# Third pair's weight sums, late x blocks and the typed stretch's x sums at other steps

## The reference, cut to what matters

```
x = x + L0(x)   # three shared relu MLPs 256->1024->256 on all tokens, two experts per batch chosen by its type,
                # a gate from the batch's first token mixes expert, s0, s1, s2
x = x + L1(x)   # eight weighted experts and one shared: (silu(x Wg) * (x Wu)) Wd, 256->1024->256
x = x + L2(x)   # adapter by language, 256->64->256, then layernorm
x = x + L3(x)   # matrix by subject, 256->256
```

## Time and profile before

| | |
|---|---|
| median of 3 runs | 1608.95 us (1607.98 to 1612.6) |
| the profiled execution's own time | 1607.21 us |
| its span | 1605.4 us, mean granted clock 0.997 |
| PE busy | 1583.1 us (99%), 7944 matmuls |
| PEld / DVE / ACT / POOL busy | 84% / 71% / 58% / 41% |

### The profile page before, as it was taken

One profiled execution on the slowest core, in us unless ns is written; L12 is line 12 of the kernel. 1 busy time (PEld: TensorE's weight loads), 2 busy tenths in 40 slices (PEclk: granted clock), 3 DMA queues, 4 the chain that ended last, 5 costly groups with the idle time before them and its releaser, 6 DMA issues.

```text
span 1605.4 us, 22399 instructions
## 1 busy us (share of the span) xinstructions
PE 1583.1 (99%) x7944; PEld 1346.5 (84%) x7944; DVE 1132.4 (71%) x1676; ACT 930.0 (58%) x1680; POOL 658.2 (41%) x576
## 2 busy tenths in 40 slices
PE   8999999999999999999999999999999999999999
PEld 6788888999897888888888888888888888888888
DVE  5665556788888776776776776776776777656556
ACT  4555554665666666666656656666666566554343
POOL 7665553745755441341341341341441431146110
PEclk9999999999999999999999999999999999999999
DMA  4111104555431010010010010010010010022000
GB/s 158 53 53 53 53 27 158 171 171 168 153 114 40 14 40 27 13 41 27 14 40 27 14 40 27 14 40 27 13 40 27 14 40 27 27 55 54 13 14 27
DMA packets 30500, 85.46 MB, mean 53 GB/s; under 512 B 5030, under 2 KB 10022, under 8 KB 30262
## 3 DMA queue, kind: packets, MB, share of 16 engines
q1 hardware_dynamic: 29798, 82.68, 15.7%
q0 software_dynamic: 304, 1.10, 0.2%
q10 hardware_dynamic: 288, 0.26, 0.1%
HBM read 81.93 MB, written 2.10 MB: 52 GB/s over the span
## 4 chain that ended last, share of the span: by engine, by line
PE 94%; DVE 3%; POOL 1%; issue 1%; ACT 1%; DMA 0%; SPq 0%; ACTq 0%; DVEq 0%; POOLq 0%
PE up L668 13%; PE up L669 13%; PE up L670 13%; PE sum L435 12%; PE sum L437 12%; PE sum L436 12%; PE up L435 4%; PE up L437 3%; PE up L436 3%; PE up L445 2%; PE up L443 2%; PE up L444 2%; DVE expert_out L2006 1%; DVE x L1988 0%; DVE hidden L2020 0%
## 5 line engine op out<-in xcount | busy, mean ns | idle before, releaser
L1267 ACT ACTIVATE hidden_hi<-up_tile 128x512 fp32r<-128x512 f32 x256 | 161.2, 630 | 187.3 <-DVE up_tile L2064 163.3
L2059 DVE TENSOR_TENSOR gate_tile<-up,gate_tile 128x512 f32<-128x512 f32 x192 | 130.0, 687 | 141.8 <-PE up L670 141.7
L2069 DVE TENSOR_TENSOR hidden_lo<-up_tile,hidden_hi 128x512 fp32r<-128x512 f32 x256 | 196.6, 787 | 44.7 <-ACT hidden_hi L1267 44.7
L668 PE MATMUL up<-x_sums,gate_up 128*128 128x512 f32 x512 | 199.3, 389 | 0.0
L437 PE MATMUL sum<-hidden_hi,down 128*128 128x512 f32 x512 | 199.2, 389 | 0.0
L435 PE MATMUL sum<-hidden_hi,down 128*128 128x512 f32 x512 | 199.2, 389 | 0.0
L436 PE MATMUL sum<-hidden_lo,down 128*128 128x512 f32 x512 | 199.2, 389 | 0.0
L670 PE MATMUL up<-x_sums,gate_up 128*128 128x512 f32 x512 | 199.2, 389 | 0.0
L669 PE MATMUL up<-x_sums,gate_up 128*128 128x512 f32 x512 | 199.2, 389 | 0.0
L2064 DVE TENSOR_TENSOR up_tile<-up_tile,gate_tile 128x512 f32<-128x512 f32 x192 | 183.5, 982 | 2.3
L1260 ACT ACTIVATE gate_tile<-gate_tile 128x512 f32<-128x512 f32 x192 | 119.8, 633 | 90.3 <-DVE gate_tile L2059 88.2
(11 more groups left out here) (323 smaller groups left out, 3956.9 us busy)
## 6 DMA issues: line engine op xcount, KB each, us to landing
raw<-in_experts SPq DMA_DIRECT2D x64, 512.0 KB, 3.3
raw<-in_l SPq DMA_DIRECT2D x51, 512.0 KB, 3.3
raw<-in_shared SPq DMA_DIRECT2D x23, 512.0 KB, 3.3
raw<-in_w SPq DMA_DIRECT2D x8, 256.0 KB, 2.6
x<-in_xT SPq DMA_DIRECT2D x3, 512.0 KB, 9.1
l_stage<-in_l SPq DMA_DIRECT2D x3, 512.0 KB, 4.6
out<-out_stage SPq DMA_DIRECT2D x6, 256.0 KB, 2.8
gate_w<-in_gw POOLq DMA_DIRECT2D x1, 1024.0 KB, 5.1
```

Of the source, the lines that this page charges most:

```text
L668: pe.matmul(out, wh, vh, start=first, stop=False, skip_group_check=True)
L1267: A(hi[:, i], cu[:, i], ACT.Copy).then_inc(hi_done, 1)
L2059: V.tensor_tensor(t, ps, t, ALU.add).then_inc(c_done[m], 1)
L2069: V.tensor_tensor(lo[:, i], cu[:, i], hi[:, i].bitcast(f32), ALU.subtract).then_inc(lo_done, 1)
```

## The change

Six edits of order. No instruction is added or taken away on a computing engine, and no DMA.

1. ACT: `shared_up_hi(1)` stands before `plain_hi(5)` in place of behind it.
2. POOL: for pair 2 the order is `shared_sums(2)`, then the four `shared_x_sum(1, i)`, then `shared_up_lo(2)`, `shared_down_lo(2)`. Before, the four x sums stood ahead of `shared_sums(2)`.
3. ACT: in slots 2 and 3 the high part of an x block stands before the high part of the weights, and block 3 comes first, then block 2.
4. VectorE: the low part of block 3 is made in slot 3 and that of block 2 in slot 5 (before: block 2 in slot 2, block 3 in slot 3).
5. TensorE: at a = 12 both low parts of x are waited for at the "first" products.
6. Typed stretch: POOL's two low parts of mixed x for tb = 1 go from q = 36, 37 to 38, 39, for tb = 2 from q = 52, 53 to 57, 58; the four x sums from q = 48 to 51 to 53 to 56; their low parts from q = 56 to 59 to 59 to 62. ACT's high parts of these sums go from steps 5, 7, 9, 11 of the last block to 11, 13, 15, 17, and the table load from step 13 to 19.

```diff
@@ TensorE, shared_up
                     if a == 12:
-                        pe.wait_ge(xin_lo, 1)
+                        pe.wait_ge(xin_lo, 2)
...
                 if part == "fourth":
-                    if a == 12:
-                        pe.wait_ge(xin_lo, 2)
@@ ACT, start
             for i in range(2):
                 shared_x_hi(0, i)
+            shared_up_hi(1)
             plain_hi(5)
-            shared_up_hi(1)
             plain_hi(6)
@@ ACT, shared_slot
+                if a in (2, 3):
+                    x_in_hi(5 - a)
                 if a % 2 == 0 and a + 2 < NA:
                     shared_up_hi(a // 2 + 1)
                 elif a % 2 == 1 and a + 1 < NA:
                     shared_down_hi((a + 1) // 2)
                 if a == 3:
                     vec_exp()
-                if a in (2, 3):
-                    x_in_hi(a)
@@ ACT, last block of the typed stretch
-            hooks = {n: [lambda i=i: xt_hi_part(0, i)] for i, n in enumerate((5, 7, 9, 11))}
-            hooks[13] = [silu_table]
+            hooks = {n: [lambda i=i: xt_hi_part(0, i)] for i, n in enumerate((11, 13, 15, 17))}
+            hooks[19] = [silu_table]
@@ POOL, start
                 shared_sums(p)
+                if p == 2:
+                    for i in range(4):
+                        shared_x_sum(1, i)
                 shared_up_lo(p)
                 shared_down_lo(p)
-                if p == 1:
-                    for i in range(4):
-                        shared_x_sum(1, i)
@@ POOL, typed stretch
-                    AFTER[EX_CH * (tb + 1) + 4 + dt] = lambda tb=tb, dt=dt: mixed_lo_part(tb, dt)
+                    AFTER[EX_CH * (tb + 1) + (6 if tb == 1 else 9) + dt] = lambda tb=tb, dt=dt: mixed_lo_part(tb, dt)
...
-            AFTER[LAST_BLOCK] = first_x_sum
+            AFTER[LAST_BLOCK + 5] = first_x_sum
             for i in range(1, 4):
-                AFTER[LAST_BLOCK + i] = lambda i=i: x_sum(0, i)
+                AFTER[LAST_BLOCK + 5 + i] = lambda i=i: x_sum(0, i)
             for i in range(4):
-                AFTER[LAST_BLOCK + 8 + i] = lambda i=i: x_sum_lo(0, i)
+                AFTER[LAST_BLOCK + 11 + i] = lambda i=i: x_sum_lo(0, i)
@@ VectorE
             def x_in_lo(b):
-                dve.wait_ge(xin_hi, b - 1)
+                dve.wait_ge(xin_hi, 4 - b)
...
-                if a in (2, 3):
-                    x_in_lo(a)
+                if a in (3, 5):
+                    x_in_lo(3 if a == 3 else 2)
```

## The result

| | before | changed |
|---|---|---|
| median | 1608.95 us (5 runs, 1607.98 to 1613.15) | 1599.09 us (5 runs, 1596.85 to 1600.63) |
| profiled execution's own time | 1607.21 us | 1598.26 us |
| its span | 1605.4 us | 1596.5 us |

The ratio is 0.993, with a 95% interval of 0.9912 to 0.9948. Forecast were 1597.5 us and a range of 1594 to 1601.5.

The account below looks back on a forecast made before the run. TensorE, busy 1583.1 of 1605.4 us, was taken as the bound, so only its gaps could be won. Gains of 7.3 + 0.5 + 1.5 + 1.3 = 10.6 us from 1608.1 gave 1597.5 us, range 1594 to 1601.5.

Parts of the forecast that it names:

- The long gap: Start, TensorE's 5.66 us gap before the matmul at 42.89: edits 2, 3 and 4 win 7.3 us (6.0 to 8.2).
- The new wait: Start, a = 2: TensorE would wait for VectorE's hidden low part, 0.2 to 1.1 us, taken as 0.9.
- "no wait" for POOL's low part: Start, a = 4: pair 2's low part ready at 43.5 to 45.5, wanted at 45.5; wait 0 to 1, taken as 0.
- a wait on `shared_up` near 45: Start: TensorE waiting there on POOL's `shared_up` was listed as a sign that the prediction was wrong.
- the first rival: Start: POOL's low part comes near 46.5, TensorE waits 1 us; sum 8.4, total 1599.7 us; chance 0.12.
- The clock in the gap: Start, to slot 4: 2.1 of the 8.2 us lost was put on matmuls at the lower clock.
- Edit 1: Start: ACT's `shared_up_hi(1)` starts 0.8 us earlier, with POOL's low part and a matmul following; 0.5 us won (-0.3 to +0.9).
- Block 2: Typed stretch: moving POOL's low parts two chunks later shrinks the 1.67 us gap to about 0.1; 1.5 us won (0.9 to 1.7).
- The new place: Block 2, steps 9 to 12: VectorE has one mix instruction in two chunks there; charged 0.1 us.
- Block 3: Typed stretch: gaps of 3.36 us go, ten chunks with a second POOL instruction cost 2.1 more; 1.3 us won (-1.8 to +2.7).
- The clock rival: A short fall of TensorE's clock comes or goes with shifted times, worth 2.1 us: 1595.5 or 1599.5; chance 0.08.
- the price moves with the work: Typed-stretch rival: moved POOL work keeps its price except where VectorE has slack; sum 6.9, total 1601.2 us; chance 0.12.

Follow-up runs that it names:

- e3: Changed kernel with POOL's four x sums ahead of pair 2's weight sums again; 1605.74 us, one time.
- e4: Changed kernel with VectorE's low parts of x blocks 3 and 2 made in slots 2 and 3; 1599.86 us, one time.
- e7: Changed kernel without edit 1 (shared_up_hi(1) behind plain_hi(5) again); 1598.79 us, one time.
- e9: Changed kernel with small gate matmuls spread into block 0, POOL's typed-stretch extras one per chunk without mix work, the rest behind the last chunk; 1596.51 us.
- e11: e9 with POOL's low part of mixed x block 2 moved behind the low part of layer L1's fourth gate/up weights; 1597.93 us.
- e12: e11 with the same POOL low part moved later, behind the low part of the down weights, near 491 us; 1597.14 us.
- e5: Changed kernel with ACT's x blocks in slots 3 and 4, POOL's x sums between pair 2's low parts, typed-stretch extras paired behind chunks without mix work; 1597.38 us.
- e1: Changed kernel with edit 6 undone (edits 1 to 5 only); 1601.14 us, ratio 0.9958 to the kernel before.
- e10: Changed kernel with POOL's low parts of mixed x back at q = 36, 37, 52, 53 and x sums at 54 to 57; 1601.21 us, one time.
- e2: Kernel before with edit 6 alone; 1608.64 us (11 runs), ratio 0.9995.
- e6: e5 with the 12 small gate matmuls moved from block 1 to steps 13 and 17 of block 0; 1596.32 us.
- e8: Changed kernel with only the 12 small gate matmuls moved to steps 13 and 17 of block 0; 1597.97 us, one time.

## Why the prediction was right, step by step

- **The long gap: 7.3 forecast, 6.8 measured.** The chain was the one read from the earlier trace rows; e3 shows POOL's link and e4 VectorE's. The new wait was put at 0.9 and was 0.61, and "no wait" for POOL's low part was 0.48: with the slower restarts behind them 1.4 against 0.9. POOL ended at 46.4, where I had 43.5 to 45.5 and took no wait; that is the half microsecond. Three times of POOL's were mis-sized: the weight sums ended at 34.5, where I had 32.7 (POOL had waited 1.11 for ACT and its first sum took 1.21 in place of 0.73), the x sums took 5.6 for 5.4, and the low part 6.4 for 5.4. The prediction had named a wait on `shared_up` near 45 as a sign of being wrong. It came, half a microsecond long, at 46.59: the first rival was half true, and POOL is what holds slot 4 now.
- **The clock in the gap: 2.1 forecast to return.** It did (0.52 to 1.00).
- **Edit 1: 0.5 forecast; 0.8 up to a = 2 and nothing by slot 4 at an equal start (e7 against e9), 1.27 up to a = 2 in the profile.** I let VectorE's x sum low parts eat a share of the lead. They did stretch, 3.19 us for the first two, but POOL's four pieces took 5.4 us as before. What ate it came later: the hidden low part beside POOL, and POOL's own low part. I added edit 1 to the long gap as if both counted in full, and they overlap. Together I had 7.8. The two rows give 8.1 in the profile, with late first matmuls, and 7.4 in e9 and e11, with early ones. That 7.8 lies between is in part luck.
- **Block 2: 1.5 forecast, 0.92 measured.** The 1.67 gap went. Two things were mis-sized. Against e9, which has no gap in this block, the block takes 1.27 more before and 0.35 more in the changed kernel. The old gap cost 1.6 at its place, but 0.3 of it was regained further on in the block. The new place was charged 0.1 and cost 0.5 at its place, with a wait of 0.30 on `expert_out` at 377, and 0.35 by the block's end. A second POOL instruction beside a chunk with mix work costs 0.5, also here.
- **Block 3: 1.3 forecast, 0.89 measured.** Seven gaps of 0.29 to 0.33, as many as chunks with mix work, none in the three without. Each costs 0.5 with its restart, where I had 0.3 for every chunk: 3.4 over the block (40.64 against 37.26 in e9, which has none) against 3.0. What went was right: the block before stands 4.27 above e9, and I had 3.36 and 0.9. The count was right and the price too low, because idle time leaves out the slower first matmuls after a gap.
- **What the sum did not hold:** -1.9 us in the first matmuls (-0.9 of it left by slot 4, e9 against the changed kernel) and +0.9 in block 1. The clock rival had named a fall that comes or goes, not these places, and it had not seen that the trace before already has one in block 1, 3.4 us from 320.1, too short for the page's slices of 40 us. The span fell by 8.9; the rows of the change alone make 9.9, against 10.6 forecast, and 9.2 with the start of e9. The median came out 1.6 us above the forecast.
- **The Trainium skill's rule** (page "SBUF — State Buffer", section "Who interferes with whom": VectorE instructions with two inputs in SBUF and GpSimd reads exclude each other for a whole instruction). The traces agree: 3.61 in e11 beside 1.54 in e9, with 2.37 of POOL at the same time. Read as "the price moves with the work" it also fits e11 and e12, where the price came back at the new place. It was not the likeliest case because some chunks do have slack, and there, as e9 shows in blocks 2 and 3, TensorE pays nothing.

## What to carry to other kernels

Where an engine works through a list, look at what each waiting instruction has behind it: here work wanted 90 us later, put one place too early on POOL, held ACT, then VectorE, then TensorE, and the same chain held TensorE at two other places (pair 3 in e5, the weight sums in e9). When the bound engine is 99% busy, compare the start of its n-th instruction between two traces: that shows gains of 0.1 us by stretch, where the whole time only tells 0.3%. Follow a gain to the next wait before you add it up: edit 1's 0.8 us were gone a dozen us later. Before moving work to "free" time on an engine that collides with another, list what the other one does in that window.

## What the runs showed of the hardware

The lower clock after a stretch of small matmuls was not expected. In block 1, 24 passes of 8 columns (12 matmuls) and 8 of 2 columns stand in a row of 3.5 us. Nine profiled executions have that row (before, changed, e1 to e5, e7, e10). In eight the granted clock fell to its lower level (1.2 GHz): in six 0.7 to 1.2 us behind the row and for 3.4 us, in two (e2, e3) before the row's end and for 6.8 us. In one, the changed kernel's, it did not. It cost 0.9 to 2.5 us on the same matmuls. In the five executions with the row split in two and put among full matmuls (e6, e8, e9, e11, e12) it never fell there. A gap of 1.7 us did not always bring it down: before kept its clock behind the gap that ends at 420.45, e1 lost it at 415.9, behind the same gap, which ends at 414.18 there. The window of e1:

```profile
414.00:421.00 7.00, 6.82 (x44) 6.83 (x45) 6.28 (x14) 3.64 (x9) 2.75 (x3) 0.76 0.22 75
```

The first matmuls differ too. From 7 us on they start 0.23 us apart in five executions (before, e5, e7, e9, e11), where the first row of the table is 15.1 to 15.5 us. In the nine others they start 0.43 apart, as in the gap at half clock, for 2 to 4 us, and the row is 17.0 to 17.2. The edits do not decide it, since e9 and e12 have the same start. The row ends with a wait for VectorE's first low part of x, so not all of the difference need be TensorE's own pace. In 7.5 to 10.5 us the kernel before started 15 and the changed one 8. The windows of before, of the changed kernel and of e12:

```profile
7.50:10.50 3.00, 3.00 (x15) 2.43 (x14) 2.41 (x5) 2.17 (x4) 0.67 (x1) 1.00 1.05 395
```

```profile
7.50:10.50 3.00, 3.00 (x8) 2.32 (x7) 1.52 (x4) 1.14 (x3) 0.51 (x1) 1.00 1.05 397
```

```profile
7.50:10.50 3.00, 3.00 (x8) 2.30 (x7) 2.00 (x4) 1.13 (x3) 0.52 (x1) 0.50 1.06 400
```

The changed kernel's trace holds no record of the clock before 10.7 us, and the view then prints 1.00. e12 has the same eight starts with a granted clock of 0.50 beside them, so that the changed kernel also ran at the lower level there is inferred from the pace.

These two together, up to 2.1 and 2.5 us, are of the size of the spread of one kernel's runs (3.8 us in the changed one). That they make all of it was not shown.
